# A window-attention and spiking-layer kernel: where the group norm's small steps stand, how q reaches its stacks, and loops written out

## The chip, the cores and the metric

The kernel runs on one core of one Trainium2 chip. The metric is the device time of one execution in microseconds; the times below are medians over repeated executions. Five engines work side by side, each with its own stream of instructions: TensorE (PE, with its weight loads shown as PEld), VectorE (DVE), ScalarE (ACT), GpSimd (POOL) and SyncE (SP), which here only issues transfers. They meet only through semaphores.

## The reference

`x` is [8, 32, 32, 256]. It is normalised in 32 groups of channels per sample, goes through window attention (windows of 8x8, 16 heads of 16 channels, a bias table and a mask), is added to x, is normalised again, and goes through a linear layer whose output charges neurons over the sample axis:

```python
def _gn(v, G=32, eps=1e-05):
    g = v.reshape(B_, H_, W_, G, C_ // G)
    m = jnp.mean(g, axis=(1, 2, 4), keepdims=True)
    s = jnp.var(g, axis=(1, 2, 4), keepdims=True)
    return ((g - m) / jnp.sqrt(s + eps)).reshape(v.shape)
...
qkv = (part @ qkv_w.T + qkv_b).reshape(n * NW, WS, 3, N_HEAD, HEAD_DIM)
q, k, v = (qkv[:, :, 0] * SCALE, qkv[:, :, 1], qkv[:, :, 2])
attn = jnp.einsum('wihd,wjhd->whij', q, k)
attn = softmax(attn.reshape(...) + bias[None, None] + MASK[None, :, None])
out = jnp.einsum('whij,wjhd->wihd', attn, v)
...
h = jnp.einsum('tbld,hd->tblh', x, W) + b          # x is here the normalised sum
v = v + (x_t - v) / 2;  s = (v >= 1);  v = v * (1 - s)   # over the 8 samples
...
x = x + attention(_gn(x))
x = x + lif(_gn(x))
```

## The kernel before, in words

Channels lie on the partitions, in two halves of 128. A sample has 4 rows of windows (32 rows in all, each of 4 windows or 256 tokens); a row is worked as two **pairs** of windows, so there are 64 pairs, 8 per sample. `k` is the number of the pair in its sample, 0 to 7; pair numbers below are this k. Each engine runs a function `pair(n, row, k, s)` through `run`, which writes out sample 0 and samples 5 to 7 and runs samples 1 to 4 in a hardware loop of two turns, two samples in each. The order of the instructions in the text is the order on each engine.

What a pair does on the path that matters here:

- In an odd pair TensorE first makes q and k of the row two further on (`project_q`, `project_k`; they read `xn_hi` and `xn_lo`). ScalarE writes their high halves (`q_high`, `k_high`), VectorE the low ones (`q_low`, `k_low`). SyncE then moves them (`move_q_and_k`): each part is spilled to DRAM and read back into `q_stack` and `k_stack`, which hold the heads as the score products need them. Rows alternate between slot 0 and slot 1.
- `scores`: 16 products of bias and 16 of q and k in each half, then 16 small ones with the row maxima (line 1026). Ahead of the last product of q and k (line 1016) TensorE waits for `max_rows` and for the stack that the **next** pair needs. In an odd pair that is the next row's, and so a new one.
- `max_scores` of the next pair, `weigh_values` of the pair before, `turn_attention`. In an even pair v is projected first.
- GpSimd writes the low half of the probabilities (`p_lo`, line 457), adds the attention to x (line 446), and in even pairs writes `xn_lo` of the row three on (`low_part`, line 415).

The **norm of the next sample** runs beside this in stages: VectorE's moments (line 705), TensorE's average over groups (`average_means`, line 911, in pair 0), VectorE's means and spreads, TensorE's second average (line 915, pair 1), VectorE's first guess of the root, then 13 small instructions of GpSimd (`norm_roots`, lines 230 to 238) whose last ends `norm_ready`. ScalarE waits for that in pair 3, ahead of `q_high`, to normalise the next sample's first row. `norm_beside` says which stage stands in which pair. Sample 1's norm is wholly done before pair 0 of sample 0.

After the pairs come 32 units of the spiking layer (`lif_units`, in `over_y`: four times eight, the middle two in a hardware loop).

Of the kernel before, what the change touches and what calls it, by code (L numbers as in the profile page):

```python
# [6 lines left out]
def swin_attention_then_lif_kernel(nc, image, x, qkv_w, qkv_b, bias_table, lif_w, lif_b, out):  # L7
# [29 lines left out]
    QUADS = 4  # L37
# [10 lines left out]
    with ctx:  # L48
# [46 lines left out]
        q_spill = [[nc.dram_tensor(f"q_spill{i}{part}", [32, QUADS, HALVES * ROWTOK], f16).ap() for part in ("hi", "lo")] for i in range(2)]  # L95
# [56 lines left out]
        q_hi_spilled = sem("q_hi_spilled")  # L152
        q_lo_spilled = sem("q_lo_spilled")
# [96 lines left out]
        def over_y(eng, body):  # L250

            body(0)
            with eng.Fori(1, WROWS - 1) as y:
                body(y)
            body(WROWS - 1)

        BODY = 2 * WROWS
        STACKS = 13 * 16
# [33 lines left out]
        def _(sp):  # L292
# [18 lines left out]
            def stack_q(slot, first, part):  # L311
                sp.dma_start(q_stack[slot][first:first + 32, :, :, :].rearrange("r g n i -> r (g n i)"),  # L312
                             q_spill[slot][part].rearrange("r g n -> r (g n)")).then_inc(stacked[slot], 16)
# [8 lines left out]
            def move_q_and_k(slot, r):  # L322

                sp.wait_ge(q_flat_done, r + 1)
                spill(q_flat, 0, q_hi_spilled, q_spill[slot][0])
                sp.wait_ge(k_hi_done, r + 1)
                spill(k_flat, 0, k_hi_spilled, k_spill[slot][0])
                sp.wait_ge(k_lo_done, r + 1)
                spill(q_flat, 1, q_lo_spilled, q_spill[slot][1])
                if not is_first(r, 2):  # L330
                    sp.wait_ge(score_ps_done, 4 * (r - 2) + 4)
                spill(k_flat, 1, k_lo_spilled, k_spill[slot][1])
                sp.wait_ge(q_hi_spilled, (r + 1) * 16)
                stack_q(slot, 32, 0)
                stack_q(slot, 64, 0)
# [4 lines left out]
                sp.wait_ge(q_lo_spilled, (r + 1) * 16)  # L340
                stack_q(slot, 0, 1)
# [32 lines left out]
        def _(pool):  # L374
# [65 lines left out]
            norm_roots(pool, root_pool, 0, 1, HALVES, HALVES)  # L440
# [7 lines left out]
            def pair(n, row, k, s):  # L448
                p = k % 2
                if p == 0 and not is_last_row(row, 2):  # L450
                    low_part(k // 2 % 2, row + 3)

# [10 lines left out]
                norm, first, width, stage = norm_beside(s, k)  # L463
                if stage == 1:
# [14 lines left out]
        def _(act):  # L479
# [162 lines left out]
        def _(dve):  # L642
# [175 lines left out]
            dve.wait_ge(const_step, 11)
            v_low(1, 2)
# [350 lines left out]
```

## Time and profile before

| | us |
|---|---|
| median of 3 runs (lowest, highest) | 541.38 (540.62, 543.15) |
| the profiled execution | 540.94 |
| its span, first to last instruction | 539.2 |
| PE busy (mean granted clock 0.946) | 435.4 (81%) |
| DVE, ACT, POOL busy | 405.2, 379.0, 279.8 |
| POOL p_lo line 457, 128 of them | 148.1 |
| DVE: two `bn_stats`, two moments, one bias table | 0.75, 0.38, 1.95 to 2.16 |
| ACT: q's or k's high half of a row | 0.84 |
| from the last `p_lo` (469.05) to the end | 70.15 |
| largest PE waits after the start | on xn_lo 16.2, on the moments 12.7, on k_stack transfers 16.5 |

Busy time is that of one engine; the engines overlap. No engine is busy all the time, so the waits between them have to be read: the view of waits names for each idle stretch what ended it. Of PE's clock the profile shows the granted share, 1.0 or 0.5 of full speed.

### The profile page before, as it was taken

The page shows a single profiled execution, that of the slowest core. Times are in us where ns is not written, and L with a number is a line of the kernel's source. Part 1 is how long each engine was busy: PE and PEld are TensorE (multiplying, and loading weights), DVE is VectorE, ACT ScalarE, POOL GpSimd, SP SyncE. Part 2 cuts the span into 40 slices and gives each one's busy share as a digit, 9 for nine tenths or more (in the row PEclk, how much of TensorE's full clock was granted, in tenths as well). Part 3 has the DMA queues.
Part 4 walks back from the last instruction along what each step waited for, and adds up shares of the span by engine and source line. Part 5 has one row for each costly group of instructions (what it writes and reads, how often), then busy time and mean ns, then how long its engine had stood idle before and what let it go on. Part 6 is the DMA issues. An engine that isn't in the chain of part 4 may idle for free.

```text
span 539.2 us, 20239 instructions
## 1 busy us (share of the span) xinstructions
PE 435.4 (81%) x7848; PEld 402.3 (75%) x7848; DVE 405.2 (75%) x872; ACT 379.0 (70%) x895; POOL 279.8 (52%) x382
## 2 busy tenths in 40 slices
PE   0346769887888786979887987987798889689997
PEld 0345768887878785978787977987797778578886
DVE  8863658787768675768786889786767787489888
ACT  3372578887878685768886988886787786665551
POOL 5453646666655665356665666755665555740000
PEclk9995889999989898889998999998999998899999
DMA  7144225454554354435554545554435443023333
GB/s 225 48 120 116 72 68 139 116 143 119 128 121 123 107 133 106 120 88 133 128 136 111 132 105 137 134 126 102 100 79 120 117 124 60 2 79 137 136 136 137
DMA packets 137802, 61.57 MB, mean 114 GB/s; under 512 B 108530, under 2 KB 126196, under 8 KB 137716
## 3 DMA queue, kind: packets, MB, share of 16 engines
q1 hardware_dynamic: 137376, 60.33, 42.7%
q8 instruction: 64, 1.05, 0.9%
q14 instruction: 22, 0.18, 0.1%
q10 hardware_dynamic: 340, 0.01, 0.0%
HBM read 35.13 MB, written 25.17 MB: 112 GB/s over the span
## 4 chain that ended last, share of the span: by engine, by line
PE 26%; SPq 20%; issue 15%; POOL 12%; DVE 10%; ACT 9%; DMA 8%; POOLq 1%; ACTq 0%; DVEq 0%
SPq L318 14%; POOL p_lo L457 5%; SPq L312 4%; PE pv_ps L1050 3%; PE proj_ps L928 3%; PE pv_ps L928 3%; PE score_ps L928 3%; DMA q_spill0hi<-q_flat 3%; DMA k_stack<-k_spill0lo 2%; POOL xc L446 2%; PE proj_ps L939 2%; ACT v_hi L531 2%; PE max_ps L928 2%; PE proj_ps L941 2%; PE proj_ps L940 2%
## 5 line engine op out<-in xcount | busy, mean ns | idle before, releaser
L457 POOL TENSOR_TENSOR p_lo<-probs,p_hi 128x512 f16<-128x512 f32 x128 | 148.1, 1178 | 151.4 <-ACT p_hi L614 113.9
L1016 PE MATMUL score_ps<-q_stack,k_stack 96*128 96x64 f16 x1024 | 87.9, 196 | 30.6 <-ACT max_rows L604 11.5
L613 ACT ACTIVATE probs<-score_ps 128x512 f32<-128x512 f32 x128 | 76.9, 601 | 44.2 <-PE score_ps L1026 40.6
L787 DVE TENSOR_REDUCE neg_max<-max_ps 128x16 f16<-128x1024 f32 x64 | 78.4, 1225 | 33.3 <-PE max_ps L996 31.9
L939 PE MATMUL proj_ps<-xn_hi,w_hi 128*128 128x256 f32 x256 | 80.5, 314 | 26.3 <-POOL xn_lo L415 16.2
L1016 PEld LDWEIGHTS score_ps<-q_stack,k_stack 96*128 96x128 f16 x1024 | 73.5, 100 | 37.7 <-ACT max_rows L604 19.0
L1012 PE MATMUL score_ps<-both_parts,bias_k 128*128 128x64 f16 x1024 | 80.1, 196 | 0.0
L781 DVE TENSOR_TENSOR v_lo<-proj_ps,v_hi 64x256 f16<-64x256 f32 x128 | 54.2, 423 | 32.4 <-ACT v_hi L531 30.8
L614 ACT ACTIVATE p_hi<-score_ps 128x512 f16<-128x512 f32 x128 | 77.3, 604 | 0.0
L940 PE MATMUL proj_ps<-xn_lo,w_hi 128*128 128x256 f32 x256 | 75.7, 296 | 0.0
L941 PE MATMUL proj_ps<-xn_hi,w_lo 128*128 128x256 f32 x256 | 75.7, 296 | 0.0
L939 PEld LDWEIGHTS proj_ps<-xn_hi,w_hi 128*128 128x128 f32 x256 | 52.7, 206 | 30.4 <-POOL xn_lo L415 17.9
L1012 PEld LDWEIGHTS score_ps<-both_parts,bias_k 128*128 128x128 f16 x1024 | 72.1, 100 | 2.7 <-issue 0.2
L531 ACT ACTIVATE v_hi<-proj_ps 64x256 f16<-64x256 f32 x128 | 50.5, 394 | 15.6 <-PE proj_ps L951 13.9
L1050 PE MATMUL pv_ps<-v_hi,p_hi 128*128 128x68 f16 x512 | 57.9, 200 | 3.5 <-POOL p_lo L457 3.5
L1050 PE MATMUL pv_ps<-v_lo,p_hi 128*128 128x68 f16 x512 | 57.6, 198 | 0.0
L1050 PE MATMUL pv_ps<-v_hi,p_lo 128*128 128x68 f16 x512 | 57.4, 198 | 0.0
L1050 PEld LDWEIGHTS pv_ps<-v_hi,p_hi 128*128 128x128 f16 x512 | 50.2, 102 | 8.8 <-POOL p_lo L457 4.1
L802 DVE TENSOR_TENSOR attn<-pv_ps,recip 64x256 f32<-64x256 f32 x128 | 54.0, 422 | 3.0
L940 PEld LDWEIGHTS proj_ps<-xn_lo,w_hi 128*128 128x128 f32 x256 | 52.7, 206 | 0.0
L941 PEld LDWEIGHTS proj_ps<-xn_hi,w_lo 128*128 128x128 f32 x256 | 52.5, 205 | 0.0
L1050 PEld LDWEIGHTS pv_ps<-v_hi,p_lo 128*128 128x128 f16 x512 | 50.1, 100 | 0.0
(130 smaller groups left out, 1193.0 us busy)
## 6 DMA issues: line engine op xcount, KB each, us to landing
xc<-in_x_dram SPq DMA_DIRECT2D x32, 256.0 KB, 3.4
out_dram<-xc SPq DMA_DIRECT2D x32, 256.0 KB, 2.0
q_stack<-q_spill0hi SPq DMA_DIRECT2D x32, 128.0 KB, 2.6
q_stack<-q_spill1hi SPq DMA_DIRECT2D x32, 128.0 KB, 2.7
q_spill0hi<-q_flat SPq DMA_DIRECT2D x16, 128.0 KB, 3.3
k_spill0hi<-k_flat SPq DMA_DIRECT2D x16, 128.0 KB, 3.2
q_spill0lo<-q_flat SPq DMA_DIRECT2D x16, 128.0 KB, 2.7
k_spill0lo<-k_flat SPq DMA_DIRECT2D x16, 128.0 KB, 2.6
```

The source lines that it names most:

```text
L318: sp.dma_start(k_stack[slot][rows, quads, :, e * WS:(e + 1) * WS], k_spill[slot][part][e * D:(e + 1) * D, quads, :].rearrange("d g (n j) - ...
L457: pool.tensor_tensor(p_lo[p][:, quads, :, :].rearrange("p g w i -> p (g w i)"), probs[:, quads, :, :].rearrange("p g w i -> p (g w i)"), p ...
L531: last = act.activation(v_block(v_hi[slot], w, e), v_part(w, e), ACT.Copy)
L613: act.activation(probs[:, quads, :, :].rearrange("p g w i -> p (g w i)"), score_ps[:, h, :], ACT.Exp)
L614: act.activation(p_hi[p][:, quads, :, :].rearrange("p g w i -> p (g w i)"), score_ps[:, h, :], ACT.Exp)\
L787: dve.tensor_reduce(neg_max[:, :].rearrange("p (m n) -> p m n", m=2)[:, :, 0:8], max_ps[:, :, :].rearrange("p m (n j) -> p m n j", j=WS), ...
L939: pe.matmul(dst, w_hi[:, c, cols], high[:, tok], start=(c == 0), stop=False)
L940: pe.matmul(dst, w_hi[:, c, cols], low[:, tok], start=False, stop=False)
L941: last = pe.matmul(dst, w_lo[:, c, cols], high[:, tok], start=False, stop=(c == HALVES - 1))
L1012: pe.matmul(dst, bias_k[:, variant(k, w), h * QUADS + 2 * mid + q, :], both_parts[:, 0, :], start=(h == 0 and q == 0 and w == 0), stop=False)
L1016: pe.matmul(dst, k_stack[slot][0:96, 2 * mid + q, at, :], q_stack[slot][0:96, 2 * mid + q, at, :], start=False, stop=False)
L1050: last = pe.matmul(cols[:, :, g, :], pp[p][:, g // 2 * 4 + h * 2 + g % 2, :, :].rearrange("p w i -> p (w i)"), vv[k // 2][:, p, h * QUADS ...
```

## The change

Five edits:

1. **Moments in pair 7.** VectorE computes the moments of sample s + 2 in pair 7 of sample s, right behind that pair's `attention_out`, where it did so in pair 0 of sample s + 1. The `bn_stats` of x that an odd pair does stand ahead of `attention_out` now and no longer at the pair's end.
2. **Roots behind xn_lo.** GpSimd's 13 instructions go from the end of pair 1 to pair 2, behind `low_part` and ahead of `p_lo`.
3. **q's parts moved together.** `q_flat`'s high and low halves go out in one transfer of 256 KB once `k_low` is done; they come back in two (64 partitions and 32) in place of three.
4. **Sample 1's averages in pairs 0 and 1** of sample 0, as for all other samples, and not in the set-up.
5. **No hardware loops**: `run` and `over_y` are written out.

```diff
         def run(eng, body):
-            for k in range(BODY):
-                body(k, k // 2, k, 0)
-            with eng.Fori(0, (SAMPLES - 3) // 2) as twice:
-                for s in (twice * 2 + 1, twice * 2 + 2):
-                    for k in range(BODY):
-                        body(s * BODY + k, s * WROWS + k // 2, k, s)
-            for s in range(SAMPLES - 3, SAMPLES):
+            for s in range(SAMPLES):
                 for k in range(BODY):
                     body(s * BODY + k, s * WROWS + k // 2, k, s)
...
-                return s + 1, (s + 1) * HALVES, HALVES, -1 if is_first(s, 1) else k
+                return s + 1, (s + 1) * HALVES, HALVES, k
...
+            def spill_q(slot):
+                sp.dma_start(q_spill[slot].rearrange("t r g n -> (r g) t n"), q_flat[:, :, :]).then_inc(q_spilled, 16)
...
             def move_q_and_k(slot, r):
-                sp.wait_ge(q_flat_done, r + 1)
-                spill(q_flat, 0, q_hi_spilled, q_spill[slot][0])
                 sp.wait_ge(k_hi_done, r + 1)
-                spill(k_flat, 0, k_hi_spilled, k_spill[slot][0])
+                spill(k_flat, HI, k_hi_spilled, k_spill[slot][0])
                 sp.wait_ge(k_lo_done, r + 1)
-                spill(q_flat, 1, q_lo_spilled, q_spill[slot][1])
+                spill_q(slot)
                 if not is_first(r, 2):
                     sp.wait_ge(score_ps_done, 4 * (r - 2) + 4)
-                spill(k_flat, 1, k_lo_spilled, k_spill[slot][1])
-                sp.wait_ge(q_hi_spilled, (r + 1) * 16)
-                stack_q(slot, 32, 0)
-                stack_q(slot, 64, 0)
+                spill(k_flat, LO, k_lo_spilled, k_spill[slot][1])
                 sp.wait_ge(k_hi_spilled, (r + 1) * 16)
                 ...
-                sp.wait_ge(q_lo_spilled, (r + 1) * 16)
-                stack_q(slot, 0, 1)
+                sp.wait_ge(q_spilled, (r + 1) * 16)
+                stack_q(slot, slice(0, 64), q_spill[slot].rearrange("t r g n -> (t r) (g n)"))
+                stack_q(slot, slice(64, 96), q_spill[slot][HI].rearrange("r g n -> r (g n)"))
...
# GpSimd: pair
                 if p == 0 and not is_last_row(row, 2):
                     low_part(k // 2 % 2, row + 3)
+                if stage == 2 and has_sample(s, 1):
+                    norm_roots(pool, root_pool, (norm - 1) * ROOT_STEPS, norm, first, width)
...
-                if stage == 1:
+                if stage == 1 and not has_sample(s, 1):
...
# VectorE: pair
-                if k == 0 and has_sample(s, 1) and not is_first(n, 1):
-                    norm_moments(norm, x_stats, 1)
...
+                if p == 1 and has_sample(s, 2):
+                    dve.wait_ge(x_loaded, row * 16 + (WROWS + 1 if k == BODY - 1 else WROWS + 2) * 16)
+                    measured = row_stats(x_stats, k // 2, row + 2 * WROWS)
...
                     attention_out(n - 1, (k - 1) % 4, beside)
+                elif beside:
+                    beside()
+                if k == BODY - 1 and has_sample(s, 2):
+                    norm_moments(s + 2, x_stats, 1)
...
# TensorE: before the pairs
-            average_means(1, HALVES, spare_averages)
             project_v(1, 1)
-            average_variances(1, HALVES, spare_averages)
```

SyncE's issues for one row in slot 1, before (the two lines of `x` loads around them left out):

```order
45 L309 DMA q_spill1hi<-q_flat 128x512 [waits q_flat_done]
46 L309 DMA k_spill1hi<-k_flat 128x512 [waits k_hi_done]
47 L309 DMA q_spill1lo<-q_flat 128x512 [waits k_lo_done]
48 L309 DMA k_spill1lo<-k_flat 128x512 [waits score_ps_done]
49 L312 DMA q_stack<-q_spill1hi 32x2048 [waits q_hi_spilled]
50 L312 DMA q_stack<-q_spill1hi 32x2048
51 L318 DMA k_stack<-k_spill1hi 16x32x64 [waits k_hi_spilled]
52 L318 DMA k_stack<-k_spill1hi 16x32x64
53 L318 DMA k_stack<-k_spill1hi 16x16x64 x4
54 L312 DMA q_stack<-q_spill1lo 32x2048 [waits q_lo_spilled]
55 L318 DMA k_stack<-k_spill1lo 16x16x64 [waits k_lo_spilled]
56 L318 DMA k_stack<-k_spill1lo 16x16x64 x3
```

The row in slot 0 that comes next, now (both slots have the same order, before and now):

```order
50 L301 DMA k_spill0hi<-k_flat 128x512 [waits k_hi_done]
51 L304 DMA q_spill<-q_flat 128x2x512 [waits k_lo_done]
52 L301 DMA k_spill0lo<-k_flat 128x512 [waits score_ps_done]
53 L312 DMA k_stack<-k_spill0hi 16x32x64 [waits k_hi_spilled]
54 L312 DMA k_stack<-k_spill0hi 16x32x64
55 L312 DMA k_stack<-k_spill0hi 16x16x64 x4
56 L307 DMA q_stack<-q_spill 64x2048 [waits q_spilled]
57 L307 DMA q_stack<-q_spill 32x2048
58 L312 DMA k_stack<-k_spill0lo 16x16x64 [waits k_lo_spilled]
```

A row has 15 issues in place of 17; behind the spill of k's low half stand 12 in place of 13, and the first of them is of k and not of q.

GpSimd from the end of pair 1 into pair 2, before (register instructions between left out; `tiny` are the steps of the roots, `rstd` and `shift` their results):

```order
71 L457 TENSOR_TENSOR p_lo<-probs,p_hi 128x512
73 L446 TENSOR_TENSOR xc<-xc,attn_cm 128x2x128
75 L230 TENSOR_TENSOR tiny<-root_guess 128x2
...
98 L236 TENSOR_TENSOR rstd<-tiny 128x2
101 L238 TENSOR_TENSOR shift<-neg_mean,rstd 128x2
```

and what followed was `xn_lo` (line 415) and `p_lo` of pair 2. Now, in sample 0:

```order
34 L405 TENSOR_TENSOR xn_lo<-xn,xn_hi 128x512 [waits xn_hi_done,bias_lo_done]
35 L223 TENSOR_TENSOR tiny<-root_guess 128x2 [waits norm_dve]
...
46 L229 TENSOR_TENSOR rstd<-tiny 128x2 [waits root_pool]
47 L231 TENSOR_TENSOR shift<-neg_mean,rstd 128x2 [waits root_pool]
48 L449 TENSOR_TENSOR p_lo<-probs,p_hi 128x512 [waits p_hi_done,pv_ps_done]
```

`xn_lo` has gone ahead of the 13 instructions; `p_lo` of pair 2 still stands behind both.

## Rows read from the trace of the kernel before

**Rows 1.** PE's waits: engine, output, line <- releaser: us in total, times, longest.
```profile
PE proj_ps L939 <- POOL xn_lo L415: 16.2, 7, 2.7
PE pv_ps L911 <- DVE moments L705: 12.7, 8, 4.9
PE score_ps L1016 <- DMA k_stack<-k_spill1lo: 8.5, 6, 1.9
PE proj_ps L949 <- issue: 4.3, 1, 4.3
```

**Rows 2.** Busy windows, samples 1 to 6: length, engines' busy us, PEclk, DMA share, GB/s.
```profile
107.72:158.78 51.06, 43.24 (x914) 40.25 (x911) 39.25 (x87) 40.12 (x99) 31.22 (x41) 0.97 0.53 129
158.78:211.40 52.62, 44.04 (x935) 40.88 (x933) 40.72 (x91) 41.69 (x102) 31.23 (x43) 0.97 0.49 121
211.40:269.09 57.69, 49.20 (x974) 46.22 (x975) 40.05 (x89) 41.51 (x102) 31.21 (x43) 0.91 0.46 113
269.09:319.22 50.13, 44.66 (x946) 41.73 (x943) 40.02 (x89) 40.98 (x101) 31.22 (x42) 0.97 0.51 126
319.22:369.92 50.70, 43.28 (x919) 40.34 (x915) 39.93 (x88) 40.42 (x99) 31.23 (x43) 0.97 0.53 129
369.92:422.74 52.82, 46.15 (x975) 43.20 (x974) 37.99 (x82) 41.81 (x103) 31.22 (x43) 0.97 0.41 97
```

**Rows 3.** The same view, at the loop's turn and in the spiking layer.
```profile
212.80:219.50 6.70, 5.70 (x77) 5.46 (x81) 1.44 (x4) 2.18 (x6) 0.50 (x1) 0.50 0.41 72
484.00:532.00 48.00, 48.00 (x247) 42.95 (x246) 43.94 (x69) 26.41 (x51) 0.00 (x0) 1.00 0.36 136
```

**Rows 4.** Timeline of PE, sample 2: start us, us, line, operation [idle before <- releaser].
```profile
154.67 0.32 PE L1026 MATMUL score_ps<-max_rows,pick_max 64*64 64x128 f16 x4
...
168.39 0.42 PE L1026 MATMUL score_ps<-max_rows,pick_max 64*64 64x128 f16 x16
...
177.89 0.39 PE L939 MATMUL proj_ps<-xn_hi,w_hi 128*128 128x256 f32 x1 [2.65 <-POOL xn_lo L415]
...
183.83 0.36 PE L1026 MATMUL score_ps<-max_rows,pick_max 64*64 64x128 f16 x12
...
196.01 0.19 PE L1016 MATMUL score_ps<-q_stack,k_stack 96*128 96x64 f16 x1 [1.47 <-DMA k_stack<-k_spill1lo]
196.13 0.42 PE L1026 MATMUL score_ps<-max_rows,pick_max 64*64 64x128 f16 x16
...
207.52 0.25 PE L1026 MATMUL score_ps<-max_rows,pick_max 64*64 64x128 f16 x3
```

**Rows 5.** Timeline of SyncE's issues behind the scores of pair 7, sample 1.
```profile
155.38 0.32 SPq L309 DMA_DIRECT2D k_spill1lo<-k_flat  x1
155.82 0.83 SPq L312 DMA_DIRECT2D q_stack<-q_spill1hi  x2
156.69 3.35 SPq L318 DMA_DIRECT2D k_stack<-k_spill1hi  x6
...
160.58 2.66 SPq L318 DMA_DIRECT2D k_stack<-k_spill1lo  x4
```

**Rows 6.** The page's DMA issues: count, KB each, median us from issue to landing.
```profile
q_spill0hi<-q_flat SPq DMA_DIRECT2D x16, 128.0 KB, 3.3
k_stack<-k_spill0lo SPq DMA_DIRECT2D x64, 32.0 KB, 2.2
q_spill1hi<-q_flat SPq DMA_DIRECT2D x16, 128.0 KB, 1.8
```

**Rows 7.** Timeline of GpSimd, pairs 1 and 2 of sample 2.
```profile
172.92 0.21 POOL L230 TENSOR_TENSOR tiny<-root_guess 128x2 f32<-128x2 f32 x1
...
176.57 1.27 POOL L415 TENSOR_TENSOR xn_lo<-xn,xn_hi 128x512 fp32r<-128x512 f32 x1
```

**Rows 8.** Timeline of ScalarE, pair 3 of sample 2.
```profile
176.87 0.60 ACT L492 ACTIVATE xn<-xc,shift,rstd 128x256 f32 x1 [0.34 <-POOL shift L238]
...
183.29 0.28 ACT L604 ACTIVATE max_rows<-max_ps 128x128 f16<-128x128 f16 x1
```

More of the change, by code:

```diff
@@ L94, in swin_attention_then_lif_kernel @@
         k_stack = [sb(f"k_stack{i}", [128, QUADS, HALVES * WCOLS, 128], f16) for i in range(2)]
-        q_spill = [[nc.dram_tensor(f"q_spill{i}{part}", [32, QUADS, HALVES * ROWTOK], f16).ap() for part in ("hi", "lo")] for i in range(2)]
+        q_spill = [nc.dram_tensor(f"q_spill{i}", [2, 32, QUADS, HALVES * ROWTOK], f16).ap() for i in range(2)]
         k_spill = [[nc.dram_tensor(f"k_spill{i}{part}", [32, QUADS, HALVES * ROWTOK], f16).ap() for part in ("hi", "lo")] for i in range(2)]
@@ L250, in over_y @@
         def over_y(eng, body):
-            body(0)
-            with eng.Fori(1, WROWS - 1) as y:
+            for y in range(WROWS):
                 body(y)
-            body(WROWS - 1)
         BODY = 2 * WROWS
-        STACKS = 13 * 16
+        LO, HI = 0, 1
+        STACKS = 12 * 16
         W_SCALES = ((0, C, QK_SCALE), (C, 2 * C, 1.0), (2 * C, 3 * C, 1.0))
@@ L309, in spill, with stack_q @@
                 sp.dma_start(kept.rearrange("r g n -> (r g) n"), flat[:, part, :]).then_inc(spilled, 16)
-            def stack_q(slot, first, part):
-                sp.dma_start(q_stack[slot][first:first + 32, :, :, :].rearrange("r g n i -> r (g n i)"),
-                             q_spill[slot][part].rearrange("r g n -> r (g n)")).then_inc(stacked[slot], 16)
+            def spill_q(slot):
+                sp.dma_start(q_spill[slot].rearrange("t r g n -> (r g) t n"), q_flat[:, :, :]).then_inc(q_spilled, 16)
+            def stack_q(slot, rows, kept):
+                sp.dma_start(q_stack[slot][rows, :, :, :].rearrange("r g n i -> r (g n i)"), kept).then_inc(stacked[slot], 16)
             def stack_k(slot, first, part, quads):
@@ L513, in with_bias @@
                     tok = slice(h * ROWTOK, (h + 1) * ROWTOK)
-                    last = act.activation(flat[:, 0, tok], proj_ps[:, first // 2, tok], ACT.Identity,
+                    last = act.activation(flat[:, HI, tok], proj_ps[:, first // 2, tok], ACT.Identity,
                                           bias=b_cols[:, first + h:first + h + 1])
@@ L519, in q_high @@
                 act.wait_ge(q_ps_done, done)
-                wait(act, q_hi_spilled, 16 * (done - 1))
+                wait(act, q_spilled, 16 * (done - 1))
                 with_bias(q_flat, 0).then_inc(q_flat_done, 1)
@@ L767, in q_low @@
                 dve.wait_ge(q_flat_done, done)
-                wait(dve, q_lo_spilled, 16 * (done - 1))
+                wait(dve, q_spilled, 16 * (done - 1))
                 low_with_bias(q_flat, 0).then_inc(q_lo_done, 1)
@@ L814, in _ @@
             k_low(2)
+            dve.wait_ge(const_step, 11)
+            v_low(1, 2)
             sample_stats(1)
             dve.wait_ge(x_stats_done, 2)
+            maxima(0)
             norm_moments(1, x_stats, 1)
[L818 to L823 removed]
             def pair(n, row, k, s):
@@ L835, in pair @@
                     k_low(row + 3)
-                if k == 0 and has_sample(s, 1) and not is_first(n, 1):
-                    norm_moments(norm, x_stats, 1)
                 if stage == 0 and not has_sample(s, 1):
```

25 lines of the change are left out of this document (9 added, 16 removed).

## The prediction, as it was made

> **What bounds the kernel now.** I read the waits of TensorE first, since it is the busiest engine, then windows cut at the end of each sample's last `p_lo`, then one sample's timelines. A pair number is its k in the sample; "score end" is the first product of line 1026 in an odd pair.
>
> TensorE's waits in the samples are of three kinds [rows 1]: on `xn_lo` (16.2 us, 7 times), on the moments (12.7 us, 8 times), on the stacks that SyncE's transfers fill (8.5 us in slot 1 and about as much in slot 0). A fourth happens once, 4.3 us of "issue". Samples 1 to 6 take 51.06, 52.62, 57.69, 50.13, 50.70 and 52.82 us [rows 2]; without the third their mean is 51.5. The third holds the loop's turn: both its samples 1 and 2 are done and the loop goes back. Samples 5 and 6 are straight code already and no faster than 1 and 4, so the loop costs nothing but at its turn. Sample 2 is seen in four steps from score end to score end [rows 4]: pair 7 to pair 1 13.7 us (154.67 to 168.39), 1 to 3 15.4, 3 to 5 12.3, 5 to 7 11.4.
>
> What sets these steps. In steps 3 to 5 and 5 to 7 it is SyncE. Its last spill, that of k's low half, waits for the score end of the odd pair; behind it stand 13 issues, and the next score end waits for the last of them to land. In [rows 5]: spill at 155.38, last stack issue done at 163.24, 7.9 us; 2.2 us to land [rows 6]; with the 0.7 us from score end to spill 10.8. Other rows have one issue of 1 to 2 us more, so 11 to 12.5. TensorE's wait of 1.47 us at 196.01 is this [rows 4]; 12.30 less 1.47 leaves 10.8 for its own work. In step 1 to 3 it is GpSimd: `xn_lo` starts at 176.57, behind the roots, and TensorE waits 2.65 us for it [rows 4, 7].
>
> **Edit 5, the loops.** The third sample is 57.69 against 51.5, so 6.2 us: 4.3 us of "issue" [rows 1], and PE at clock 0.50 from 212.8 to 219.5 [rows 3]. All is gone if nothing replaces it: −6.2. The bounds are 0 (the code is fetched with the same stall somewhere) and −6.2. In the spiking layer TensorE is busy 48.00 of 48.00 us across a loop's turn [rows 3], so the writing out of `over_y` gives nothing. The Trainium skill (Runtime: NRT & Kernel Launch, Instruction fetch mechanics) says that fetch runs ahead only in sequence and a taken branch out of the window stalls; the trace agrees with its 4.3 us, and straight code should then have no such stall.
>
> **Edit 4, the set-up.** TensorE waits 4.9 us for sample 1's moments ahead of the v projection, the longest of its waits on moments [rows 1]. Without that, v is done some 5 us earlier; VectorE does v's low part and sample 1's statistics before the first maxima, and I get pair 0 4.9 us earlier. Part is given back on VectorE, which gates pairs 1 and 2 through the bias tables: means and spreads in pair 0 (about 0.7), and in pair 1 the statistics (0.75) and the variance (0.5) ahead of the table. Then GpSimd: roots of 3.6 us stand in pair 2 of sample 0 behind a late `low_part`, and ScalarE waits for them in pair 3. Left: 4.9 − 0.7 − 1.25 − 1.5 = 1.4. Value −1.4, bounds +1 (the roots end another 2.5 later) and −4.9.
>
> **Edit 1, the moments.** TensorE's wait is 12.7 less the 4.9 of the set-up, over 7: 1.1 us each, six of them in samples 1 to 6 in pair 0 [rows 1]. VectorE's two moments go into pair 7, where it has idle time behind `attention_out`. The `bn_stats` (0.75 us per odd pair) now stand ahead of `attention_out`; behind that wait only the attention's turning on TensorE a pair later, more than 3 us away. If that slack were gone it would be 0.75 per row, 3 us per sample.
>
> **Edit 2, the roots.** They take 172.92 to about 176.55, 3.6 us [rows 7]. With `xn_lo` (1.2 us) ahead of them, it ends near 174.2 and TensorE does not wait. The roots end at 177.8, 1.2 us later than before, and `p_lo` of pair 2 starts at 177.8, where `xn_lo` ends now. What is late next: ScalarE in pair 3. It waits for the roots, normalises (0.6), does q (0.84), normalises, does k, then `max_rows`: before 176.87 to 183.29, waiting for the projections in between [rows 8]. Now 177.85 + 0.6 + 0.8 + 0.6 + 0.8 gives `max_rows` at 180.8. The step 1 to 3 is 13.0 in place of 15.4, of which some 1.5 was work at half clock after the 2.65 us stall: a sample's mean clock of 0.97 [rows 2], at levels of 1 and 0.5, is about 3 us at the lower one, and half of that is lost. Without that loss the step would have been 13.9. TensorE still idles about 1.5 us there and may still lose its clock in half the samples, so 13.5.
>
> **Edit 3, q's transfers.** Behind the score end stand 12 issues in place of 13; one costs 0.42 to 0.49 with its gap, from 0.83 for two [rows 5]. The other issue saved lies ahead of the score end, where SyncE waits anyway. The wait for the first spill stays: k's high half is now issued where q's was, and a spill in slot 0 lands after 3.3 us, in slot 1 after 1.8 [rows 6]. So −0.5 per row that SyncE bounds: steps 3 to 5 and 5 to 7 about 11.3 and 11.4 on the mean. Step 7 to 1, 13.7, loses the moments (1.1) and one issue (0.5); the 0.7 left above 11.4 is half-clock work behind pair 7's stall, which shrinks, so I put it at the same bound: 11.4. The new 256 KB spill must land before the six k stacks are issued, 0.4 + 3.4 us and the wait for k later; 1.8 to 3.3 for 128 KB makes that hold. By the Trainium skill (DMA: Bandwidth & Descriptors, Anatomy of one DMA) a transfer has about 2 us fixed and bytes over 436 GB/s, so doubling the bytes adds 0.3 us; the two medians above for equal bytes show that what is queued ahead weighs more.
>
> **The sum.** A sample: 11.4 + 13.5 + 11.3 + 11.4 = 47.6 for 51.5, −3.9, six times: −23.3. Loop −6.2, set-up −1.4, two rows each of samples 0 and 7 that SyncE bounds at 0.5: −2.0. Together −32.9 on the profiled execution's 540.94 gives 508.0. The median of the runs lies 0.4 above that execution, so 508.5; I say 508. The tail of the spiking layer, 70 us, stays.
>
> **Rivals.**
> A, *the stacks give nothing back*: the extra time of one issue per row is SyncE waiting for descriptors or earlier transfers to drain, and a removed issue only makes that wait longer. For it: the six-issue groups last 3.35 with 0.63 and 0.45 us issues mixed, and the last four 2.66 [rows 5]. Steps are then 12, 13.5, 12, 12 = 49.5: −2.0 × 6 − 6.2 − 1.4 = −19.6, 521.
> B, *all is freed*: the stacks arrive ahead and TensorE's own 10.8 holds in three steps, with 13.0 in the fourth: 45.4, −6.1 × 6 = −36.6, with the rest 495. Against it: SyncE still has 15 to 17 issues per row.
> C, *slower: q's spill comes too late*. It is issued only when `k_low` is done and carries both halves. If in slot 0 it lands after 7.0 us, a little over twice the 3.3 [rows 6], q's stacks wait 7.0 − 4.3 = 2.7 us, and k's low stacks behind them, in each of some 15 rows: 40 us against the gain of 33, 548. It decides from 2.2 us per row on. For it: q's high half no longer travels while SyncE waits for `k_low`. Against it: slot 1 lands in 1.8, so the queue is not full by itself.
> D, *the loop's stall stays*, since the straight stream is fetched just as late: 514. It lies within the forecast's range.
>
> **Chances.** Forecast with D 0.58 (502 to 515), A 0.24 (515 to 525), B 0.13 (under 502), C 0.05. The range 496 to 523 leaves out the end of B, the end of A and C. The measurement tells 0.5%, 2.7 us, from no change; only C and its neighbourhood reach that side: faster 0.95, same 0.01, slower 0.04.
>
> **What would show it.** No PE wait on "issue" and no 57 us sample. No `pv_ps L911` wait on the moments except in sample 7, no `proj_ps L939` wait on `xn_lo` of 2.6 us, and in its place `xn L492` of ScalarE waiting for `shift L238` 1 to 2 us once per sample. PE's waits on `k_stack` in all odd pairs, under 1 us. If SyncE shows waits on `q_spill`, C is at work; if its issues of 1 to 2 us get longer, A. Wrong altogether would be samples of 51 us with the old waits gone.

## The result, and the profile after

The changed kernel takes 513.71 us (median of four, 512.19 to 514.99) where the kernel before took 541.00 beside it (537.86 to 543.15): a ratio of 0.950, 95% interval 0.945 to 0.955. Measured again later it took 517.1, ratio 0.944 (0.938 to 0.949). The forecast was 508.0, 496 to 523. The profiled execution took 513.70 us, its span is 511.96. Throughout, the medians take in every execution and the ratios leave out those over 1.5% above a kernel's fastest, so that the two can differ by half a per cent, and the two traces of such executions (edit 3 taken back, the first time, and sample 0's roots earlier) are read in the last section alone.

TensorE's waits in the kernel after: engine, output, line <- releaser, us in total, times, longest.

```profile
PE score_ps L1004 <- ACT max_rows L595: 16.7, 27, 4.5
...
PE score_ps L1004 <- DMA k_stack<-k_spill1lo: 12.2, 12, 2.3
PE score_ps L1004 <- DMA k_stack<-k_spill0lo: 10.0, 8, 2.2
...
PE pv_ps L899 <- DVE moments L696: 1.5, 1, 1.5
```

The three waits of [rows 1] that the change aimed at are gone: none on `xn_lo` (16.2 us), one of 1.5 us on the moments (12.7), no "issue" of 4.3. What remains has grown: the waits on k's stacks, 8.5 us in slot 1 before, are 12.2 now. Over the whole span `max_rows` of ScalarE leads, but 10.4 of its 16.7 us lie outside samples 1 to 6. Within them (107.32 to 395.83) the stacks lead by far:

```profile
PE score_ps L1004 <- DMA k_stack<-k_spill0lo: 9.8, 7, 2.2
PE score_ps L1004 <- DMA k_stack<-k_spill1lo: 9.2, 10, 2.3
PE score_ps L1004 <- ACT max_rows L595: 6.3, 19, 1.2
```

The same view of the kernel before has 6.2, 6.8 and 2.6.

Windows between the ends of the samples' last `p_lo`, samples 1 to 7, of the kernel after (columns as in [rows 2]):

```profile
107.32:154.59 47.27, 42.98 (x946) 40.18 (x943) 40.51 (x89) 40.55 (x101) 31.21 (x42) 1.00 0.56 137
154.59:201.84 47.25, 42.91 (x946) 40.14 (x943) 40.73 (x89) 40.52 (x101) 31.18 (x42) 1.00 0.56 137
201.84:249.06 47.22, 42.97 (x947) 40.17 (x944) 40.31 (x89) 40.53 (x101) 31.22 (x42) 1.00 0.54 133
249.06:298.74 49.68, 44.58 (x946) 41.78 (x943) 40.73 (x89) 40.66 (x101) 31.20 (x42) 0.97 0.55 132
298.74:347.62 48.88, 42.91 (x946) 40.19 (x943) 40.51 (x89) 40.52 (x101) 31.23 (x43) 1.00 0.54 130
347.62:395.83 48.21, 44.57 (x946) 41.76 (x943) 37.49 (x81) 40.67 (x101) 31.17 (x43) 0.96 0.49 114
395.83:439.90 44.07, 36.87 (x833) 33.54 (x829) 31.95 (x79) 33.30 (x82) 28.93 (x41) 0.96 0.35 76
```

Samples 1 to 6 take 288.5 us for 315.0 [rows 2]. The third is as short as the first two, and in four of the six the clock never falls. The whole account: start to the end of sample 0, 107.32 for 107.72; samples 1 to 6, −26.5; sample 7, 44.07 for 46.31; from the last `p_lo` to the end 72.05 for 70.15. That is −0.4 − 26.5 − 2.2 + 1.9 = −27.2, the difference of the spans.

Steps from score end to score end, means over samples 1 to 6; to keep the loop's turn apart, the row of before leaves sample 3 out:

| pairs | 7→1 | 1→3 | 3→5 | 5→7 | sum |
|---|---|---|---|---|---|
| before | 12.85 | 14.74 | 12.07 | 11.81 | 51.47 |
| forecast | 11.4 | 13.5 | 11.3 | 11.4 | 47.6 |
| after | 11.76 | 12.71 | 11.91 | 11.71 | 48.09 |

Step 1 to 3 in sample 2. First GpSimd of the kernel after (start us, us, line, operation), then ScalarE and TensorE:

```profile
167.06 1.27 POOL L405 TENSOR_TENSOR xn_lo<-xn,xn_hi 128x512 fp32r<-128x512 f32 x1
...
171.57 0.20 POOL L231 TENSOR_TENSOR shift<-neg_mean,rstd 128x2 f32<-128x2 f32 x1
171.72 2.28 POOL L449 TENSOR_TENSOR p_lo<-probs,p_hi 128x512 f16<-128x512 f32 x2
```

```profile
171.86 0.60 ACT L483 ACTIVATE xn<-xc,shift,rstd 128x256 f32<-128x256 f32 x1 [1.36 <-POOL shift L231]
...
174.29 0.29 ACT L595 ACTIVATE max_rows<-max_ps 128x128 f16<-128x128 f16 x1
```

```profile
174.68 0.19 PE L1004 MATMUL score_ps<-q_stack,k_stack 96*128 96x64 f16 x1 [1.17 <-ACT max_rows L595]
```

Before, the 13 small instructions ran first and `xn_lo` started when they were done [rows 7]; now it ends at 168.3 and the 2.65 us stall of [rows 4] is gone. In this sample ScalarE takes over as the late one: it waits 1.36 us for the last of the roots (0.34 in [rows 8]), and `max_rows` stands 2.4 us behind the first normalising.

That is not so in every sample. The last wait of step 1 to 3 ends by `max_rows` in samples 1 and 2 (1.11 and 1.17 us), by slot 0's stack in samples 3, 5 and 6, and in sample 4 no wait is over 0.5 us:

```profile
221.42 0.19 PE L1004 MATMUL score_ps<-q_stack,k_stack 96*128 96x64 f16 x1 [1.46 <-DMA k_stack<-k_spill0lo]
...
319.00 0.19 PE L1004 MATMUL score_ps<-q_stack,k_stack 96*128 96x64 f16 x1 [1.95 <-DMA k_stack<-k_spill0lo]
...
367.63 0.19 PE L1004 MATMUL score_ps<-q_stack,k_stack 96*128 96x64 f16 x1 [1.78 <-DMA k_stack<-k_spill0lo]
```

From sample to sample the stack lands between 0.6 us before and 0.8 us behind the end of `max_rows`. In the second trace of this kernel the stack ends the wait in four of the six. So SyncE and ScalarE bound this step side by side.

SyncE behind the scores of pair 7 of sample 1, kernel after, the place of [rows 5]:

```profile
151.54 0.47 SPq L301 DMA_DIRECT2D k_spill1lo<-k_flat  x1
152.05 4.58 SPq L312 DMA_DIRECT2D k_stack<-k_spill1hi  x6
156.68 1.12 SPq L307 DMA_DIRECT2D q_stack<-q_spill  x2
157.84 1.89 SPq L312 DMA_DIRECT2D k_stack<-k_spill1lo  x4
```

I call the time from the start of the spill of k's low half to the end of the last stack issue **the issue stretch**, and the time from there until that last stack has landed **the landing**. The issue stretch is 8.2 us here for 7.9 in [rows 5], one issue fewer notwithstanding: a group of six takes 3.35 or 4.58. One row says nothing; over rows 4 to 27 of the 32 (counted from 0, here and below) the stretch is 8.58 us on the mean for 9.29. But the landing is 2.25 us for 1.52. The page's DMA issues of the kernel after, median us from issue to landing last:

```profile
q_spill<-q_flat SPq DMA_DIRECT2D x32, 256.0 KB, 2.6
q_stack<-q_spill SPq DMA_DIRECT2D x32, 256.0 KB, 3.5
...
q_stack<-q_spill SPq DMA_DIRECT2D x32, 128.0 KB, 3.6
...
k_stack<-k_spill0lo SPq DMA_DIRECT2D x64, 32.0 KB, 3.1
```

q's spill of 256 KB lands in 2.6 us, between the 3.3 and 1.8 of the halves [rows 6]; the last k stacks, 2.2 us before, take 3.1 (the page counts from the start of an issue, the landing above from its end). Issue stretch and landing together are 10.81 us before and 10.83 after. I call this sum **the chain** below.

### The profile page after: what moved, and what is told of

Same layout as the page of the kernel before. It is cut to its first block, busy times and chain, and to the rows that moved or that the text cites. A ratio compares the mean times of both kernels' runs of the same rounds, so it can differ in the third digit from the quotient of the medians.

```text
span 512.0 us, 19282 instructions
## 1 busy us (share of the span) xinstructions
PE 427.2 (83%) x7848; PEld 395.4 (77%) x7848; DVE 408.6 (80%) x872; ACT 376.0 (73%) x895; POOL 277.2 (54%) x382
## 4 chain that ended last, share of the span: by engine, by line
PE 31%; SPq 18%; ACT 14%; DMA 11%; DVE 11%; issue 8%; POOL 6%; ACTq 0%; DVEq 0%; POOLq 0%
SPq L312 13%; DMA k_stack<-k_spill1lo 4%; DMA k_stack<-k_spill0lo 3%; SPq L307 3%; PE score_ps L916 3%; PE proj_ps L927 3%; ACT k_flat L505 3%; PE pv_ps L1038 3%; PE proj_ps L916 3%; PE pv_ps L916 3%; PE score_ps L1014 3%; PE proj_ps L929 2%; PE proj_ps L928 2%; DMA k_spill0hi<-k_flat 2%; ACT v_hi L522 2%
## 5 line engine op out<-in xcount | busy, mean ns | idle before, releaser
L449 POOL TENSOR_TENSOR p_lo<-probs,p_hi 128x512 f16<-128x512 f32 x128 | 146.5, 1166 | 128.6 <-PE pv_ps L1038 69.9
L1004 PE MATMUL score_ps<-q_stack,k_stack 96*128 96x64 f16 x1024 | 86.1, 194 | 41.7 <-ACT max_rows L595 16.7
L604 ACT ACTIVATE probs<-score_ps 128x512 f32<-128x512 f32 x128 | 76.9, 601 | 45.2 <-PE score_ps L1014 44.4
L1004 PEld LDWEIGHTS score_ps<-q_stack,k_stack 96*128 96x128 f16 x1024 | 71.9, 98 | 48.7 <-ACT max_rows L595 35.1
L927 PE MATMUL proj_ps<-xn_hi,w_hi 128*128 128x256 f32 x256 | 78.8, 308 | 11.1 <-DVE w_lo L731 7.2
L1000 PE MATMUL score_ps<-both_parts,bias_k 128*128 128x64 f16 x1024 | 78.2, 194 | 0.0
L928 PE MATMUL proj_ps<-xn_lo,w_hi 128*128 128x256 f32 x256 | 73.9, 289 | 0.0
L929 PE MATMUL proj_ps<-xn_hi,w_lo 128*128 128x256 f32 x256 | 73.8, 288 | 0.0
L927 PEld LDWEIGHTS proj_ps<-xn_hi,w_hi 128*128 128x128 f32 x256 | 51.0, 199 | 14.8 <-DVE w_lo L731 7.2
L928 PEld LDWEIGHTS proj_ps<-xn_lo,w_hi 128*128 128x128 f32 x256 | 51.0, 199 | 0.0
L929 PEld LDWEIGHTS proj_ps<-xn_hi,w_lo 128*128 128x128 f32 x256 | 50.7, 198 | 0.0
```

Of the source, the lines that this page charges most:

```text
L449: pool.tensor_tensor(p_lo[p][:, quads, :, :].rearrange("p g w i -> p (g w i)"), probs[:, quads, :, :].rearrange("p g w i -> p (g w i)"), p ...
L604: act.activation(probs[:, quads, :, :].rearrange("p g w i -> p (g w i)"), score_ps[:, h, :], ACT.Exp)
L927: pe.matmul(dst, w_hi[:, c, cols], high[:, tok], start=(c == 0), stop=False)
L928: pe.matmul(dst, w_hi[:, c, cols], low[:, tok], start=False, stop=False)
L929: last = pe.matmul(dst, w_lo[:, c, cols], high[:, tok], start=False, stop=(c == HALVES - 1))
L1000: pe.matmul(dst, bias_k[:, variant(k, w), h * QUADS + 2 * mid + q, :], both_parts[:, 0, :], start=(h == 0 and q == 0 and w == 0), stop=False)
```

## The experiments

Each ran beside the kernel before. Us by the ratios are differences of ratios times the 542 us of that kernel. "After" is the mean of the changed kernel's two ratios, 0.947.

**The loops alone**: the kernel before with edit 5.

```diff
 def run(eng, body):
-    ... sample 0; a hardware loop over samples 1 to 4; samples 5 to 7
+    for s in range(SAMPLES):
...
 # over_y
-    body(0)
-    with eng.Fori(1, WROWS - 1) as y:
+    for y in range(WROWS):
```

> The kernel before with edit 5 alone (all loops written out). Theory: the third sample's 57.7 us was the loop's turn and nothing replaces it, so this kernel is 5 to 6.5 us faster than before (about 535), has no PE wait on issue, and its sample 3 takes 51 to 53 us like the others. Rival (D of the prediction): the code is fetched as late in a straight stream; the same 4 us stall and the 57 us sample stay, and the time is that of before.

535.74 us for 545.43, ratio 0.987 (0.981 to 0.993): 7.0 us, with 3.7 to 10.4 as the interval. The stall on "issue" is not in its waits. Its samples 1 to 3:

```profile
107.42:161.03 53.61, 46.17 (x915) 43.33 (x912) 40.55 (x89) 40.65 (x99) 31.24 (x42) 0.91 0.49 120
161.03:213.33 52.30, 44.70 (x973) 41.78 (x972) 40.42 (x89) 41.51 (x102) 31.29 (x42) 1.00 0.48 122
213.33:262.05 48.72, 43.13 (x946) 40.29 (x943) 40.35 (x89) 40.96 (x101) 31.30 (x43) 1.00 0.54 131
```

The third falls from 57.69 to 48.72 and no other sample has the stall: rival D is out. (The first is long by its clock, 0.91 on the mean.) The Trainium skill (Runtime: NRT & Kernel Launch, Instruction fetch mechanics) puts the stall on a taken branch and has the fetching of straight code mostly hidden; both kernels agree with it.

**Edit 3 taken back** in the kernel after: q's two spills and three stacks of before. Measured twice.

```diff
-                spill_q(slot)
+                ... spill(q_flat, HI) ahead of k's high half, spill(q_flat, LO) here
+                stack_q(slot, 32, 0); stack_q(slot, 64, 0)    # ahead of the six k stacks
...
-                stack_q(slot, slice(0, 64), ...); stack_q(slot, slice(64, 96), ...)
+                stack_q(slot, 0, 1)
```

> The changed kernel with edit 3 undone (q's halves travel apart, in the old order, 17 issues per row). Theory L (the landing takes the issue back): behind the spill of k's low half the issues again take 0.7 us longer and the last one lands 0.7 us sooner, so the time is within 2 us of the changed kernel, either way. Rival I (the issues bound, as the prediction had it): 0.5 us per row in about 26 rows, so 10 to 14 us slower than the changed kernel, 524 to 528.

521.45 us, ratio 0.958 (0.952 to 0.965). The second time:

> The changed kernel with edit 3 undone, once more, on the chip that runs the kernel with edit 3 alone. Theory P: chain 11.2 to 11.4 us, 4 to 10 us slower than the changed kernel's ratio to before of 0.944 to 0.950, so 0.953 to 0.966. Theory L: 0.945 to 0.953.

519.76 us, ratio 0.953 (0.948 to 0.959). With 0.947 for the kernel after, edit 3 is worth 0.9%, 5 us. The second trace agrees: steps of 11.75, 12.65, 12.47 and 12.28, 49.1 a sample, are 0.8 longer than the mean 48.3 of the two traces with edit 3, so 5 us in six samples. The result lies between the two theories, 2 us and 10 to 14. Its landing row:

```profile
k_stack<-k_spill0lo SPq DMA_DIRECT2D x64, 32.0 KB, 2.1
```

The issue stretch is 9.38 us and the landing 1.69, chain 11.08.

**Edit 3 alone**, on the kernel before (the diff above, turned round).

> The kernel before with edit 3 alone. SyncE's chain in the samples is the time from the issue of the spill of k's low half to the landing of the last k_stack transfer: 10.8 us in before, 10.8 in the changed kernel, 11.3 in the changed kernel without edit 3. Theory P (pace): the chain lengthens by 0.5 us when the other edits bring the rows closer together, and edit 3 takes 0.45 back at any pace; then here it is 10.3 to 10.5 us, and the kernel is 3 to 9 us faster than before. Theory L (landing): the landing of the last transfer takes the saved issue back at any pace; then it is 10.7 to 10.9 here and the time is that of before within 2.7 us.

542.54 us (12 executions) for 544.19, ratio 0.993 (0.989 to 0.997): 4 us by the ratio, 1.7 by the medians. The issue stretch is 8.53 (before 9.29) and the landing 2.22 (1.52), the chain 10.74 (10.81). So the chain comes out by theory L and the ratio by theory P; the profiled execution is no faster than that of the kernel before, 540.86 for 540.94, with a sample 0 that ends 3.3 us later. The medians of the page:

```profile
q_stack<-q_spill SPq DMA_DIRECT2D x32, 256.0 KB, 3.6
...
k_stack<-k_spill0lo SPq DMA_DIRECT2D x64, 32.0 KB, 2.9
```

So edit 3 lengthens the landing by 0.7 with or without the other edits. The gain in the chain is 0.1 us on the kernel before and 0.25 to 0.3 on the kernel after, where two traces have 10.83 and 10.78 against 11.08. The spread from kernel to kernel is as large: the loops alone, with SyncE's order of before, have 10.60. That the landing takes most of the saved issue back is shown; the idea that the pace of the rows lengthens the chain without edit 3 has only the 11.08 for it.

**q's stacks among k's**: in the kernel after, q's two read-backs go behind the first two k stacks (one `stack_k` issues two), so that they are long under way when the last four are issued.

```diff
                 sp.wait_ge(k_hi_spilled, (r + 1) * 16)
                 stack_k(slot, 0, 0, slice(0, QUADS))
-                stack_k(slot, 32, 0, slice(0, 2))
-                stack_k(slot, 64, 0, slice(2, QUADS))
                 sp.wait_ge(q_spilled, (r + 1) * 16)
                 ... the two stack_q
+                stack_k(slot, 32, 0, slice(0, 2))
+                stack_k(slot, 64, 0, slice(2, QUADS))
```

> The changed kernel with the two transfers into q_stack issued after the first two k_stack transfers and not after the sixth; the count of issues is the same. Theory L: with 384 KB of q no longer right ahead of them, the last four k_stack transfers land 0.7 us sooner after their issue (1.5 for 2.25 us), at the price of some wait for the spill of q, about 0.3 us; 5 to 12 us faster, 502 to 509. Rival (the whole queue drains at one rate, whatever the order): landing and issues together stay 10.8 us, the time is within 2 us of 513.7.

515.9 us, ratio 0.951 (0.946 to 0.956), not told apart from the kernel after: the 5 to 12 us of theory L did not come. The landing is indeed back to 1.54:

```profile
k_stack<-k_spill0hi SPq DMA_DIRECT2D x64, 32.0 KB, 3.2
k_stack<-k_spill0lo SPq DMA_DIRECT2D x64, 32.0 KB, 2.2
```

But the issue stretch is 9.12 us for 8.58, the chain 10.66. Most of what the landing gains the issues lose. The four small high stacks, now right behind q, are the ones at 3.2 (2.3 in the kernel after). The Trainium skill (DMA: Bandwidth & Descriptors, Anatomy of one DMA) gives its fixed 2 us and bytes over 436 GB/s for transfers that GpSimd issues; by it 256 KB would land 0.3 us later than 128 KB. On SyncE's queue the two q stacks of the kernel after have 3.5 and 3.6 us, so here the bytes of the transfer itself don't decide: 128 KB right behind 256 take as long as the 256.

**One more issue, same bytes**: the 64-partition q stack in two of 32 partitions.

```diff
-                stack_q(slot, slice(0, 64), q_spill[slot].rearrange("t r g n -> (t r) (g n)"))
+                stack_q(slot, slice(0, 32), q_spill[slot][LO]...)
+                stack_q(slot, slice(32, 64), q_spill[slot][HI]...)
```

> The changed kernel with the 64-partition transfer into q_stack cut in two of 32: the same bytes, one issue more per row. Rival I (the issues bound): 0.45 us per row more, 10 to 13 us slower. Theory L (what is in the queue bounds): the added issue runs while earlier transfers drain, the last landing comes 0.4 us sooner after its issue, and the time is within 2 us of the changed kernel.

517.26 us, ratio 0.952 (0.947 to 0.957). The issue stretch is 9.32 us, 0.7 above the kernel after, the landing 1.70 for 2.25: chain 11.03. An issue costs 0.7 us in the stretch and about 0.2 in the chain. In time that is 0.5% by the ratio, inside the intervals; the 10 to 13 us of rival I are out.

```profile
q_stack<-q_spill SPq DMA_DIRECT2D x96, 128.0 KB, 2.7
...
k_stack<-k_spill0lo SPq DMA_DIRECT2D x64, 32.0 KB, 2.5
```

q's read-backs land in 2.7 us each, for 3.5 and 3.6. This also shows that the bytes right ahead don't set the landing alone: the same 384 KB of q stand ahead of the last k stacks in both kernels, and the landing is 2.25 us behind two transfers and 1.70 behind three. When q lands says more. Means over the same rows, from the spill of k's low half: the last read-back of q is issued at 5.7 us in the kernel after, at 6.4 in this one and at 6.4 in the kernel before, but it lands at 9.3, 9.2 and 9.0; the last k stack lands 1.5, 1.8 and 1.8 us behind it. So the saved issue moves q's read-backs forward in SyncE's order and not in their landing, and the last stack comes behind them. What holds q's landing where it is stays open.

**The changed kernel once more**, with the next three:

> The changed kernel again, as the reference for the three beside it on this chip. Both theories: ratio to before 0.945 to 0.955.

517.1 us (510.65 to 526.33), before 542.07, ratio 0.944 (0.938 to 0.949), a little under what was expected. End of sample 0 at 106.72, steps 11.60, 12.83, 12.39 and 11.71, 48.5 a sample; chain 8.40 + 2.38 = 10.78.

**Edit 1 taken back**: moments in pair 0, `bn_stats` at the end of the odd pairs.

```diff
+                if k == 0 and has_sample(s, 1) and not is_first(n, 1):
+                    norm_moments(norm, x_stats, 1)
...
-                if k == BODY - 1 and has_sample(s, 2):
-                    norm_moments(s + 2, x_stats, 1)
```

> The changed kernel with edit 1 undone (moments back in pair 0, statistics back at the pair's end). Theory: TensorE's wait of 1.1 to 1.4 us on the moments returns once in each of samples 1 to 6 and comes on top of the step from pair 7 to pair 1: 4 to 8 us slower than the changed kernel. Rival (covered): that step is bound by the stack transfers already, so the wait only takes the place of the wait on k_stack in pair 1, and the time stays within 2 us.

519.31 us, ratio 0.958 (0.954 to 0.962): 2.2 us more by the medians, 6 by the ratios. Step 7 to 1 is 12.58 for 11.76 and 11.60, and the waits on the moments are back:

```profile
PE pv_ps L901 <- DVE moments L696: 9.1, 7, 1.6
```

Seven waits, 1.3 us each; step 7 to 1 gets back 0.9 of that per sample, about 5 us in six, as the term of 1.1 said.

**Edit 2 taken back** from sample 1 on: the roots at the end of pair 1.

```diff
-                if stage == 2 and has_sample(s, 1):
+                if stage == 2 and s == 0:
...
-                if stage == 1 and not has_sample(s, 1):
+                if stage == 1 and s > 0:
```

> The changed kernel with edit 2 undone from sample 1 on (roots at the end of pair 1; in sample 0 they stay in pair 2). Theory: TensorE waits 2.6 us for xn_lo again in samples 1 to 6, the step 1 to 3 is 13.8 to 15.3 us for 12.7, and the kernel is 8 to 14 us slower than the changed one. Rival (given back): an earlier step that ends later lets SyncE get ahead, the later steps shorten by as much, and the loss is under 5 us.

527.3 us, ratio 0.969 (0.964 to 0.974): 10.2 us more by the medians, 12 by the ratios, the largest single part. Step 1 to 3 is 14.21 for 12.71 and 12.83, and the wait is back:

```profile
PE proj_ps L927 <- POOL xn_lo L405: 15.5, 6, 2.6
```

Six waits of 2.6 us, of which the step shows 1.4: the rest is hidden by what comes late next.

**Edit 4 taken back**: sample 1's averages and roots in the set-up.

```diff
-                return s + 1, (s + 1) * HALVES, HALVES, k
+                return s + 1, (s + 1) * HALVES, HALVES, -1 if is_first(s, 1) else k
...
+            average_means(1, HALVES, spare_averages)
             project_v(1, 1)
+            average_variances(1, HALVES, spare_averages)
```

> The changed kernel with edit 4 undone (sample 1's averages and roots in the set-up). Theory Z (the set-up edit is worth nothing, as the two traces show 107.4 and 107.7 us to the end of sample 0): within 1.5 us of the changed kernel. Rival (the 1.4 us of the prediction, or more, masked by other differences of sample 0): 1.5 to 4 us slower.

520.28 us, ratio 0.960 (0.957 to 0.964): 3.2 us more by the medians, 7 by the ratios. The end of sample 0 is at 109.38. The traces with edit 4 in an unchanged set-up (the kernel after twice, edits 1 to 3 taken back one by one, q's stacks moved or split) have 105.15 to 107.66, mean 106.6: so 2.8 us, with that spread about it. The four traces without edit 4 (before, the loops alone, edit 3 alone, this one) have 107.42 to 111.02, mean 108.9, which makes it 2.3. Some of it is clock: up to the end of sample 0 the granted clock stands at 0.50 for 30.7 us in this trace, and for 20 to 27 us in the seven. TensorE's waits in it:

```profile
PE pv_ps L903 <- DVE moments L697: 6.1, 2, 4.9
...
PE pv_ps L907 <- DVE tiny L710: 3.6, 1, 3.6
```

**Sample 0's roots earlier**: in the kernel after, sample 0 alone does its roots in pair 1, ahead of the bias table, in place of behind the late `low_part`.

```diff
-                if stage == 2 and has_sample(s, 1):
+                if stage == 2 and s > 0 and has_sample(s, 1):
...
+                if n == 1:
+                    norm_roots(pool, root_pool, 0, norm, first, width)
+                    pool.wait_ge(norm_ready, 2)
```

> The changed kernel with the 13 root instructions of sample 0 in pair 1, ahead of the low half of the bias, where GpSimd idles 5 us; all other samples as changed. Theory: ScalarE no longer waits 1.3 us for them in pair 3 of sample 0, and p_lo of pair 2 starts 2 to 3 us earlier; the end of sample 0 comes 0.5 to 2 us sooner and the kernel is that much faster, at the edge of what can be measured. Rival: that pair is bound by VectorE's bias tables and ScalarE's max_rows anyway, 0.

516.64 us, ratio 0.945 (0.940 to 0.949), as the kernel after: the gain of 0.5 to 2 us that was expected doesn't show.

**The roots 0.7 us earlier in every sample**: the last one, and in samples 1 to 6 GpSimd's addition of the attention of pair 1 (`xc`, 0.72 us) goes behind the roots of pair 2.

```diff
                 if stage == 2 and s > 0 and has_sample(s, 1):
                     norm_roots(...)
+                    add_attention(n - 3, row - 2, 1)
...
-                if not is_first(n, 2):
+                if not is_first(n, 2) and not (stage == 1 and has_sample(s, 1)):
```

> As the one above, and in samples 1 to 6 GpSimd's addition of the attention (0.7 us) goes from the end of pair 1 to pair 2, behind the roots, so that xn_lo and the roots start 0.7 us sooner. Theory (the step 1 to 3 is set by the end of the roots): that step falls from 12.7 to about 12.1 us and the kernel is 3 to 5 us faster than the changed one. Rival (GpSimd then waits for xn_hi of ScalarE, or the stacks bound the step): under 1 us.

513.86 us, ratio 0.945 (0.941 to 0.949): no faster than the one above, where 3 to 5 us were expected. Sample 0 ends at 104.60, just below the lowest of the others, 105.15. ScalarE's six waits for the roots are halved, 4.0 us for 8.0. But step 1 to 3 is 12.74 for 12.71. TensorE in pair 3 of sample 2:

```profile
173.61 0.19 PE L1008 MATMUL score_ps<-q_stack,k_stack 96*128 96x64 f16 x1 [1.76 <-DMA k_stack<-k_spill0lo]
```

At the place where the kernel after waits 1.17 us for `max_rows` this one waits 1.76 for the stack, and now the stack ends this wait in all six samples, for three in the kernel after. Its waits on slot 0's stacks are 15.2 us in 13, for 10.0 in 8. So relieving ScalarE alone leaves step 1 to 3 to SyncE, which bounded half of them already.

The parts don't add up. By the ratios edit 5 alone gives 7 us, and taking back edits 1 to 4 costs 6, 12, 5 and 7: 37 us, where the whole change gives 29 (0.947). By the medians edits 1, 2 and 4 come to 2.2, 10.2 and 3.2. Each part is known to some 3 us and no better.

## Why the prediction came out as it did, step by step

The sign and the range were right, and so were the four signs on the waits of "issue", the moments, `xn_lo` and ScalarE. The fifth, waits on k's stacks of under 1 us, was not: in samples 1 to 6 they are 17 of 1.1 us on the mean, up to 2.3. The profiled execution lies 5.7 us above the forecast. By its own terms:

- **Edit 5**: forecast −6.2. Alone it gives 7.0 (3.7 to 10.4), and the third sample of the kernel after is 47.2. Right.
- **Edit 2**: forecast 13.5 for step 1 to 3, measured 12.71: the gain was put 0.8 us a sample too small. Half a us of the 13.5 stood for a lower clock in half the samples. The windows show 1.00 in four of six; but the second trace has the clock fall in four of six (48.5 us a sample for 48.1) and its step 1 to 3 is 12.83, so that half us doesn't come in this step either way. The mechanism is half of what was put: ScalarE waits for the roots as forecast, 1.36 us for 1 to 2, but `max_rows` ends the wait of the step in two samples and slot 0's stack in three. That the stack is as late as ScalarE was not foreseen.
- **Edit 1**: 1.1 us a sample forecast, 0.9 taken back by undoing it. `bn_stats` ahead of `attention_out` cost nothing that the steps show. Right.
- **Edit 3, the step that failed**: −0.5 per row that SyncE bounds. Steps 3 to 5 and 5 to 7 went from 12.07 and 11.81 to 11.91 and 11.71, not to 11.3 and 11.4, and step 7 to 1 to 11.76, not 11.4. I had taken the landing, 2.2 us, as fixed. The issues did shrink, 0.7 us for the one removed, more than the 0.5 forecast; the last landing grew by 0.7, since the last stack lands behind q's read-backs, and those, issued 0.7 us earlier, land no earlier (9.3 us behind the spill for 9.0). What is left by experiment is 4 to 5 us in all, for the 11 that my terms come to (1.5 a sample, and 2.0). The 2.2 us were also set down in the wrong place: [rows 6] counts from the start of an issue, and I added them behind its end, where 1.5 is measured; the row of [rows 5] with its 7.9 us was a short one besides, the mean is 9.29. Rival A's *stacks give nothing back* was closer for three steps, 12 each. Its mechanism, a longer wait of SyncE, is not what happens: the issue stretch is shorter, the landing longer. The steps together are 48.09 for 47.6 forecast, 2.9 us in six samples.
- **Edit 4 and samples 0 and 7**: forecast −1.4 and −2.0. Measured −0.4 to the end of sample 0 and −2.2 in sample 7, 0.8 short. Undoing edit 4 costs 2.3 to 2.8 up to there, clock included, so nothing shows the term of 1.4 to be too large; what hides it is that sample 0 spreads by 2.5 us from execution to execution. In the profiled execution the clock stood at 0.50 for 27 us of the set-up and sample 0, for 20.5 at most in the six others, and sample 0's roots ran late:

```profile
34.62:38.04 3.42, 3.42 (x18) 3.42 (x17) 0.88 (x2) 1.99 (x4) 2.14 (x1) 0.50 0.64 153
```

```profile
72.22 1.27 POOL L405 TENSOR_TENSOR xn_lo<-xn,xn_hi 128x512 fp32r<-128x512 f32 x1
...
76.74 0.20 POOL L231 TENSOR_TENSOR shift<-neg_mean,rstd 128x2 f32<-128x2 f32 x1
```

  Working `low_part` and then the roots, GpSimd is busy from 72.22 to 76.9, with `p_lo` behind. How much of sample 0's lateness is the clock and how much the roots stays open: moving the roots made no difference in the times.
- **The tail**: forecast 0, measured +1.9. The next section shows it; I had not looked for a chance event there.
- **Rival C** is out: SyncE has no wait on `q_spill` anywhere; in its place it waits for the spill of k's high half, 7.2 us in slot 0 (8 times). **Rival B** asked for stacks ahead of time, and they are the largest waits of samples 1 to 6.

The terms that missed add up: 2.9 + 0.8 + 1.9 = 5.6 of the 5.7. That the miss is so small is in part luck: the 2.9 are 7.7 us that steps 7 to 1, 3 to 5 and 5 to 7 lack in six samples, less 4.7 that step 1 to 3 gives beyond its forecast. With that step right, the sum would have been off by 10.

## What to carry to other kernels

Where a queue's issues and the last landing stand in one chain, price both: removing an issue ahead of a small transfer shortened the chain by 0.1 to 0.3 of its 0.7 us here, since the large transfers ahead of it landed no earlier. When one wait is taken out of a step, work out the next two late ones and not one alone, and in every sample rather than in one: here ScalarE and SyncE stood within 0.8 us of each other behind GpSimd, and a second edit that relieved one gained nothing. Work behind a stall can come out at either clock, so a forecast of a single execution needs that as a spread and not as a number.

## What the runs showed of the hardware that I had not expected

**The clock falls or not at one and the same place.** In the spiking layer TensorE waits 1.03 us and then 0.81 us (both within 0.01) in all 14 traces, for the same instructions. The kernel after:

```profile
445.66 0.38 PE L899 MATMUL proj_ps<-moments,group_avg 128*128 128x2 f32 x2 [1.03 <-DVE moments L696]
446.85 0.38 PE L903 MATMUL proj_ps<-tiny,group_avg 128*128 128x2 f32 x2 [0.81 <-DVE tiny L709]
...
447.30 1.57 PE L916 MATMUL score_ps<-unit,w_lif 128*128 128x256 f32 x4
...
448.88 1.91 PE L916 MATMUL score_ps<-unit,w_lif 128*128 128x256 f32 x4
```

Its windows there:

```profile
444.00:447.64 3.64, 1.80 (x10) 1.26 (x10) 2.38 (x13) 3.31 (x7) 0.40 (x1) 1.00 0.19 72
447.64:451.05 3.41, 3.41 (x11) 2.79 (x10) 2.22 (x5) 0.22 (x1) 2.56 (x10) 0.50 0.14 54
451.05:456.00 4.95, 4.95 (x26) 4.43 (x26) 4.71 (x8) 3.02 (x6) 1.01 (x4) 1.00 0.22 81
```

The kernel before, with the same two waits:

```profile
474.80 0.38 PE L911 MATMUL proj_ps<-moments,group_avg 128*128 128x2 f32 x2 [1.03 <-DVE moments L705]
476.00 0.38 PE L915 MATMUL proj_ps<-tiny,group_avg 128*128 128x2 f32 x2 [0.81 <-DVE tiny L718]
476.44 1.03 PE L928 MATMUL score_ps<-unit,w_lif 128*128 128x256 f32 x4
```

Four products take 1.03 us at the full clock (granted 1.0) and 1.91 at the half (0.50, for 3.4 us). In nine of the 14 traces the clock falls there, and from the end of the second wait to the end of the kernel it is 65.1 us; in five it stays (before, edit 3 alone, edit 2 taken back, sample 0's roots earlier, edit 3 taken back the first time), and it is 63.2 to 63.4. The code there is the same in 12 of them; the other two (before, edit 3 alone) have the hardware loop, and the full clock. Of the 12 with straight code three kept it. Whether the loop matters, or only chance, is open; it was not tried.

**A taken branch costs more than its stall**: 4.3 us of "issue", and 6.7 us at clock 0.50 behind it [rows 1, 3], together an extra 6.2 us in that sample; writing the loop out gave 7.0.
